# A two-layer graph kernel: destination counts by search, three window and pick buffers, and the source one-hots at the end of VectorE's chunk

## The reference

```python
h_proj = einsum('nd,rde->rne', h, relation_weight)          # 32 projections of each node
t_r, h_r = h_proj[etype, src], h_proj[etype, dst]
att = sum(t_r * tanh(h_r + edge_attr), axis=-1)             # softmax over the edges of one dst
h_nb = segment_sum(h[src] * softmax_by_dst(att)[:, None], dst)
x1 = layernorm(x + leaky_relu((h + h_nb) @ res_w1.T) + leaky_relu((h * h_nb) @ res_w2.T))
# second layer
feat = x1 / clip(count(src), 1)
x2 = layernorm(x1 + segment_sum(feat[src], dst) / clip(count(dst), 1))
```

## Time and profile before

| | us |
|---|---|
| median of the three runs (11364.19 to 11370.44) | 11367.19 |
| the profiled execution, its own time | 11368.67 |
| its span, first to last instruction | 11366.9 |
| GpSimd busy | 7620.3 (67%) |
| VectorE busy | 5468.0 (48%) |
| TensorE busy | 3427.3 (30%) |
| ScalarE busy | 2635.4 (23%) |
| granted TensorE clock, mean | 0.529 |

### The profile page before, as it was taken

How to read it: one execution, slowest core, us unless ns; L and a number is a source line. 1 busy time by engine, 2 the same in 40 slices (tenths; PEclk the granted TensorE clock), 3 DMA queues, 4 the chain that set the end, 5 groups by cost and what they waited for, 6 DMA issues and landing times. The chain is left out here.

```text
span 11366.9 us, 83832 instructions
## 1 busy us (share of the span) xinstructions
PE 3427.3 (30%) x19430; PEld 3091.6 (27%) x19596; DVE 5468.0 (48%) x5374; ACT 2635.4 (23%) x2315; POOL 7620.3 (67%) x8066
## 2 busy tenths in 40 slices
PE   5466666677777774111111111300000000000001
PEld 2266666666666663110010011300000000000001
DVE  4466666666666666777777777511111111111113
ACT  3211111111111112222222222322222222222221
POOL 2476666666666665656656655577777777777776
PEclk8755555555555555555555555555555555555555
DMA  9766556566665564333333333222222222222222
GB/s 359 275 168 164 165 167 166 165 165 165 166 166 164 165 164 131 104 107 108 104 103 111 104 103 102 47 52 55 52 52 52 52 52 52 52 52 54 53 52 50
DMA packets 1327104, 1319.07 MB, mean 116 GB/s; under 512 B 1051736, under 2 KB 1097720, under 8 KB 1313994
## 3 DMA queue, kind: packets, MB, share of 16 engines
q1 hardware_dynamic: 1038169, 748.56, 22.0%
q0 software_dynamic: 251552, 361.81, 14.4%
q10 hardware_dynamic: 37344, 208.28, 4.7%
HBM read 774.76 MB, written 543.26 MB: 116 GB/s over the span
## 5 line engine op out<-in xcount | busy, mean ns | idle before, releaser
L1122 POOL DMA_INDIRECT gs<-table,idx_s x3125 | 3049.7, 976 | 1881.1 <-issue 953.5
L1481 POOL DMA_INDIRECT gy<-ytab,idx x3125 | 2948.5, 944 | 1011.8 <-issue 952.0
L1425 PEld LDWEIGHTS banks<-win,pick 128*125 128x125 f32 x9900 | 2149.1, 331 | 349.5 <-issue 324.8
L1425 PE MATMUL banks<-win,pick 128*125 (+1 forms) x9900 | 2120.7, 413 | 199.5 <-DVE pick L1180 199.5
L1516 DVE TENSOR_TENSOR_SCAN run<-keep,add 128x1664 f32<-128x1664 f32 (+1 forms) x126 | 453.2, 3597 | 3013.7 <-ACT add L1546 3013.7
L1126 POOL DMA_INDIRECT gd<-table,idx_d x1375 | 1300.6, 946 | 419.0 <-issue 419.0
L1180 DVE TENSOR_TENSOR pick<-keyb,banks 128x1875 f32<-128x1875 uint8 x330 | 695.1, 2106 | 1342.7 <-PE banks L1430 1342.2
L540 PE MATMUL ps_cm<-tail,mask_m 128*128 128x64 f32 x196 | 43.6, 423 | 4004.6 <-DVE mask_m L475 4004.6
L1408 PE MATMUL banks<-hi,lo 128*128 128x98 bf16 x6250 | 506.8, 274 | 2410.7 <-DVE hi L1166 2410.7
L1408 PEld LDWEIGHTS banks<-hi,lo 128*128 128x128 bf16 x6250 | 495.7, 140 | 2423.8 <-DVE hi L1166 2423.8
L540 PEld LDWEIGHTS ps_cm<-tail,mask_m 128*128 128x128 f32 x196 | 42.3, 331 | 4005.9 <-DVE mask_m L475 4005.9
(11 more groups left out here) (242 smaller groups left out, 4518.9 us busy)
## 6 DMA issues: line engine op xcount, KB each, us to landing
proj_d<-found SPq DMA_DIRECT2D x330, 512.0 KB, 4.0
win<-table SPq DMA_DIRECT2D x660, 240.0 KB
table<-rows SPq DMA_DIRECT2D x98, 1536.0 KB, 10.7
sums<-rowbuf ACTq DMA_DIRECT2D x124, 825.0 KB, 4.6
ef<-in_edge_attr_dram SPq DMA_DIRECT2D x125, 800.0 KB, 4.6
sums<-rowbuf ACTq DMA_DIRECT2D x124, 800.0 KB, 3.5
keyb<-step_keys SPq DMA_DIRECT2D x332, 234.4 KB, 4.8
gd<-proj_d SPq DMA_DIRECT2D x70, 800.0 KB, 5.1
```

What stands on the lines that cost most here:

```text
L1122: pool.indirect_dma_start(out=gs[:, s, g, :], out_offset=None, in_=table_vec, in_offset=bass.IndirectOffsetOnAxis(ap=idx_s[:, s, g:g + 1], ...
L1425: nc.tensor.matmul(acc[k][0:MT, bass.ds(slots[t] * D, D)], pick[:, k, t * MT:(t + 1) * MT], win[:, k, bass.ds(at_w, 1), :].rearrange("p o ...
L1481: pool.indirect_dma_start(out=gy[:, s, g, :], out_offset=None, in_=ytab, in_offset=bass.IndirectOffsetOnAxis(ap=idx[:, s, g:g + 1], axis=0 ...
```

## The change

- Destination counts are no longer taken from one-hots of every edge. During setup the kernel finds for each node how many edges have a destination up to it: the first destination of each tile of 125 edges is counted with one-hots (25 small products on TensorE and two more for a prefix sum), then GpSimd fetches, for each of 98 columns of nodes, the one tile in which the node ends (98 more indirect DMAs), and VectorE compares and sums in seven groups of 14 (`search`). `ends` holds the result; `counts` takes differences of it.
- The one-hots of a chunk are those of its sources alone: 25 instead of 50, and 25 products instead of 50. They stand at the end of VectorE's chunk, behind the indices and pick 5.
- `win` and `pick` have three buffers; window b and pick b wait for walk b - 3 instead of b - 2. `found` and the accumulator keep two.
- ScalarE copies `gs` before tanh instead of behind it, and a near chunk's `ef` is copied in the chunk before it, ahead of `rowbuf`. The last chunk's two parts share one such copy.
- In setup GpSimd's indirect DMAs go three after every block from block 48 on (137 in all), and the bytes of `kk` are made at block 68.

The diff, cut to its core:

```diff
-KSLOTS = 4
+KSLOTS, WSLOTS = 4, 3
...
+                    pool.wait_ge(marks_mm, 2)
+                    pool.sem_inc(pool_past, 1)
+                    for b in range(12 * SLOTS, NB):
+                        for u in range((b - 12 * SLOTS) * 3, min((b - 12 * SLOTS + 1) * 3, UC + NB)):
+                            if u < UC:
...
+                            v = u - UC
+                            q = v // SEARCH
+                            if v == 0:
+                                pool.wait_ge(last_ready, 1)
...
+                            if q >= 2 and v % SEARCH == 0:
+                                pool.wait_ge(searched, q - 1)
...
+                                out=found_dst[:, q % 2, v % SEARCH, :], out_offset=None, in_=dst_tiles,
+                                in_offset=bass.IndirectOffsetOnAxis(ap=last_i[:, v:v + 1], axis=0)).then_inc(dst_in[q % 2], 16)
+                        duplicate(b, b % SLOTS, b // SLOTS)
...
+                    def search(q):
+                        at = slice(q * SEARCH, (q + 1) * SEARCH)
+                        dve.wait_ge(iota_done, 6)
+                        dve.wait_ge(dst_in[q % 2], 16 * SEARCH * (q // 2 + 1))
+                        link.then(nc.vector.tensor_tensor(upto_node[:, :, :], found_dst[:, q % 2, :, :],
+                                                          node_no[:, at].unsqueeze(2).to_broadcast([P, SEARCH, MT]), ALU.is_le))
+                        nc.vector.tensor_reduce(in_tile[:, at], upto_node[:, :, :], AX.X, ALU.add).then_inc(searched, 1)
...
-            lo = sb(c2, "lo", [P, 2 * G, P], BF16)
-            hi = sb(c2, "hi", [P, 2 * G, NB], BF16)
+            lo = sb(c2, "lo", [P, G, P], BF16)
+            hi = sb(c2, "hi", [P, G, NB], BF16)
...
-                        if later(b) and later(b - 1):
-                            sp.wait_ge(found_mm, b - 1)
+                        if not isinstance(b, int) or b >= WSLOTS:
+                            sp.wait_ge(found_mm, b - WSLOTS + 1)
...
-                        b, k, at = PER * c + j, j % 2, PER * s + j
+                        b, k, at = PER * c + j, j % WSLOTS, PER * s + j
...
-                        if j >= 2 or later(c):
-                            dve.wait_ge(found_mm, b - 1)
+                        if j >= WSLOTS or later(c):
+                            dve.wait_ge(found_mm, b - WSLOTS + 1)
...
-                        if not (isinstance(c, int) and c == CHUNKS - 1):
-                            hots(c + 1, link)
                         if far:
                             picks(c, s, i, 4)
...
                             edge_rows(link, c + 2, s, far)
                         if far:
                             picks(c, s, i, 5)
+                        if go_on:
+                            low_hots(c + 1, link)
+                            high_hots()
...
+                        if follows:
+                            take_ef(*follows)
                             act.wait_ge(run_ready, k + 1)
...
-                            for e in range(2):
-                                last = nc.tensor.matmul(hist[:, e * NB:(e + 1) * NB], lo[:, 2 * g + e, :], hi[:, 2 * g + e, :],
-                                                        start=False, stop=False)
+                            last = nc.tensor.matmul(hist, lo[:, g, :], hi[:, g, :], start=False, stop=False)
```

More of the change, by code:

```diff
@@ L851, in _ @@
                     nc.tensor.matmul(ps_m[:, 2, :], ones[:, :], marks[:, :], start=True, stop=True).then_inc(cum_mm, 1)
-                    part(pe, project, 9, END)
+                    pe.wait_ge(hots_ready, 2)
+                    for k in range(TILE_OF):
+                        last = nc.tensor.matmul(ps_n[:, 0, :], node_low[:, k, :], node_high[:, k, :], start=k == 0, stop=k == TILE_OF - 1)
+                    last.then_inc(marks_mm, 1)
+                    part(pe, project, 9, 11)
+                    pe.wait_ge(marks_ready, 2)
+                    nc.tensor.matmul(ps_n[:, 1, :], upto[:, :], node_marks[:, :], start=True, stop=True)
+                    nc.tensor.matmul(ps_n[:, 2, :], ones[:, :], node_marks[:, :], start=True, stop=True).then_inc(cum_mm, 1)
+                    part(pe, project, 11, END)
                     closing(project)
```

178 lines of the change are left out of this document (114 added, 64 removed).

## The result

The changed kernel took 10522.23 us (median of 4 runs, 10518.84 to 10523.03), the kernel before beside it 11365.69 us (11363.23 to 11370.44): a ratio of 0.9257, 95% interval 0.9241 to 0.9273. The profiled execution took 10518.84 us, its span is 10517.0 us. The forecast was 10505, with 10445 to 10695 as its range.

A forecast was written before the change was run, and what follows sets the result against it. A loop through VectorE held GpSimd back from its issue limit (TensorE set the far pace). 11368.67 - 517 (near) - 309 (far) - 59 (seam) - 12 (end) + 34 (setup) = 10505 us, range 10445 to 10695.

The forecast's parts named there:

- Near chunks, -517: First layer's 67 near chunks: GpSimd becomes the limit, 31.2 us a chunk instead of 38.92, saving 517 us.
- Far chunks, -309: First layer's far chunks: GpSimd becomes the limit, 64.4 us a chunk instead of 70.67, saving 309 us.
- GpSimd's floor, 64.4 a chunk: Far chunks: least time GpSimd needs for its 50 gathers, two of them about 0.9 us longer, 64.4 us.
- TensorE's sum of 60.2: Far chunks: TensorE's six walks need 4 x 8.35 + 13.7 + 13.1 = 60.2 us, under GpSimd's 64.4.
- term of 13.7 for the step of 18.69: Far chunks: TensorE's walk step that waits for `found` and a slot-number load falls from 18.69 to 13.7 us.
- rival of 68.5 us: Far chunks: TensorE's loop stays the limit at 68.5 us a chunk, total 10726 us; chance 0.10.
- TensorE's wait for pick 4: Far chunks: TensorE's 3.3 us wait for pick 4, behind the one-hots, goes; that step falls from 11.74 to 8.35.
- The seam, -59: Between far and near chunks, gathers of chunks 55 and 56: 73 us instead of 131.9, saving 59 us.
- The end, -12: Last edge gather to first node gather, 46.95 us before: shorter one-hots and two waits gone save 12 us.
- Setup, +34: Setup grows 34 us through 98 more gathers, searches and tile one-hots; bounds 0 and +80; setup rival's chance 0.10.
- The rule weighed: VectorE instructions with two SBUF inputs hold GpSimd's port throughout; by it setup loses 19 us, not 12, total 7 later.
- Dearer gathers: Rival in the first layer: densely packed gathers beside VectorE cost more, at 1.5 us each about 11630 us; chance 0.03.

## Why the prediction was right

**What bounds the kernel.** Right: a loop through VectorE held GpSimd back by 6.65 and 8 us a chunk, and with it gone GpSimd's issue rate holds both stages. With 18 gathers a chunk both stages became faster at once, so GpSimd was the limit in both.

**Near chunks, -517.** Measured -514.4. VectorE's need of 26.5 us showed as 26.53 with fewer gathers. The reasons were partly redundant, which the prediction did not say: the wait for `ef` is covered by the place of the one-hots as well as by ScalarE's order, and undoing either alone costs nothing; only both together bring the 32.8 us of the halved one-hots alone.

**Far chunks, -309.** Measured -295.0. The step that failed is GpSimd's floor, 64.4 a chunk: it was 64.63. The two long gathers a chunk were taken at 0.9 us over the usual; they were 1.1 us over (118.9 us in 108). Before, their mean excess was 0.96 (103.9 us in 108), and the 15 us between the two sums are as much as the forecast missed here. The prediction held them fixed, but they now begin earlier inside VectorE's instructions and wait for more of them.

**TensorE's sum of 60.2.** As a sum of what TensorE needs too high by 4.5, without effect, since GpSimd stood above it. The terms 8.35 and 13.1 were 8.3 and 13.06. The term of 13.7 for the step of 18.69 describes the changed kernel as it runs (13.41), but it is no need: where TensorE itself sets the pace, it is 9.37. In the changed kernel TensorE is held at pick 2 by the landing of the gather (2.7 us on the mean, at most 4.8), so its last walks fall later against ScalarE's chunk; that this is what puts the load of slot numbers behind a wait again was not tested by itself. So TensorE had 9 us to spare a chunk, not 4, and two picks or the old place of the one-hots did no harm. The rival of 68.5 us is out.

**TensorE's wait for pick 4** went, but another came: pick 2, now 131.8 us over 49 chunks, stands behind the add that waits for the landed gather. It costs nothing in far chunks. The prediction used just this (last four walks begin with pick 2) for the seam, but did not name it among the waits to be seen.

**The seam, -59.** Measured -53.6: 78.3 instead of 73. Against the 72.7 us that the prediction's terms add up to it is 5.6 more: 2.6 are the landing, 4.1 us after the next gather's start instead of the estimated 1.5; 1.8 lie in the steps, 8.85 + 9.97 + 13.41 against 8.35 + 8.35 + 13.7; 1.4 in the tanh argument behind the last walk; less 0.3 in the indices. GpSimd stood idle for 14.2 us, not 11.

**The end, -12.** Measured -14.3; ScalarE's old order alone gave back 4.4 of it, close to the 3.3 of the earlier trace rows.

**Setup, +34.** Measured +25.1 in the first profile, 28 to 33 in the others with this setup. The size was about right by two errors that cancel: the gathers and searches cost 34 to 41 instead of 28, the one-hots of the tiles nothing instead of 3 to 6, and the spreading of the `kk` gathers over all blocks, costed at nothing, stands beside a gain of 6 (45 blocks x 0.13 us, not tested by itself). That the sum came near is luck. The upper bound of +80 rested on reading the lower rate of the earlier trace rows as gathers slowing the stores; the run without search moves 368 GB/s with 39 gathers in it and the changed kernel 340, and what differs is GpSimd's wait for the stores, 116.1 us against 12.5: in the changed kernel the stores lack data. That gathers slow the stores a little as well is not excluded: from 222 to 400 us the run in which ScalarE writes the rows moves 365 GB/s and the one without the search 374, and in both some engine waits for the stores there.

**The rule weighed.** The prediction took from the earlier trace rows that a gather loses less than the whole of VectorE's instruction. That was misread. The gather had begun in the middle: it began 0.94 us before the end of L1201 and lost 0.81. In 108 cases the gather waits until the instruction ends, less 0.125 us. The Trainium skill (SBUF — State Buffer, section "SBUF: two separate sides") has it that the shared port is held for the whole of such an instruction, and for a gather that begins inside one the trace agrees with it. The page gives the lock to whichever of the two starts first; the trace does not show the other half of that: instructions that find a gather running take 1.82 to 1.83 us all the same, so they do not wait for it. The loss is smaller only where a gather happens to begin late. In setup the 137 gathers took 1.035 us on the mean, 12.5 us over 0.944 each, which is within the 10 to 13 of the prediction, but by luck and not by its 0.8 us for each instruction. Three gathers make 10.6 of the 12.5: two lose 1.8 and 1.7 us beside one of the seven comparisons each, and one, in the timeline of VectorE and then of GpSimd, loses 7.1:

```profile
318.63 5.23 DVE L997 TENSOR_TENSOR kk<-kk,base 128x4875 f32<-128x4875 f32 x1
323.89 2.70 DVE L998 TENSOR_SCALAR kk<-kk 128x4875 uint8<-128x4875 f32 x1
```

```profile
318.69 8.03 POOL L843 DMA_INDIRECT key_ab<-in_dst_dram,last_i  x1 [0.30 <-issue]
```

It begins just after L997 and ends 0.13 us after L998, so it was held over both, though L998 has a single input; the prediction priced L932, the same instruction as L997, alone. The same page, in the section "Who interferes with whom", says that an instruction of this kind was not seen to stall a DMA in a probe, and gives as an inferred reason that making descriptors needs the port's write side; here each of the 108 indirect DMAs was stalled.

**Dearer gathers.** In near chunks 1582.49/1675 = 0.945 us each, in far ones 0.988: under the limits of 0.95 and 0.99 that were set, the second only just. The rival was wrong about the one-hots: the 276 far-chunk gathers that begin inside one, which has an operand in PSUM, take 0.945 us on the mean and 0.954 at most. The mechanism that it named, L1201's, is the one that cost 105 us.

## What to carry to other kernels

When one engine's issue rate becomes the limit, undoing single edits tells little of their worth together, and taking some of that engine's work away shows every hidden limit in one run: here 26.5 and 55.7 us under 31.2 and 64.6. A step that was measured where an engine has slack is not what it needs: one step of TensorE took 13.4 us with slack and 9.4 without. And where GpSimd issues back to back, look for VectorE instructions with both inputs in SBUF: cutting them into pieces, or giving one an operand in PSUM, let the gathers through here (105 and 76 us).

## What was not expected of the hardware

In the far chunks an indirect DMA that begins inside a VectorE instruction with two SBUF inputs of 1600 elements each takes 0.944 us plus what is left of that instruction less 0.125 us, with a standard deviation of 0.003 us over 108 cases. The 93 that such an instruction found running were not lengthened, nor were seven that began within 0.04 us of its start. One begun beside pieces of 0.49 us loses 0.32 us at most. With one operand in PSUM, nothing is lost. Five pieces of 320 elements take 2.11 us together (their spans overlap) where one of 1600 took 1.83.
